# The gate projection's two halves change their place in TensorE's order, in a fused Mamba-2 and product-key expert kernel

## The reference

```python
x = layernorm(x + mamba2(x))       # in-projection, convolution, state-space scan, gate, out-projection
x = layernorm(x + peer(x))         # product-key retrieval of 64 experts per token out of 4096
# mamba2: z, xBC, dt = split(u @ W_in); xBC = silu(conv4(xBC)); y = ssd(x * dt, A * dt, B, C) + D * x
#         y = rmsnorm(y * silu(z)) * norm_scale; out = y @ W_out
# peer:   h = silu(x @ W_up.T + b_up) @ W_down.T + b_down          (width 2048, then 256)
#         q = h @ W_q.T; sim = q . keys; top 8 of 64 per head and half; top 8 of the 8 x 8 sums
#         z = silu((h . down_embed[idx]) * softmax(scores)); out = sum(z * up_embed[idx])
```

## Time and profile before

| | |
|---|---|
| runs | 3216.73, 3226.48, 3239.93 us; median 3226.48 |
| profiled execution | 3229.48 us, its span 3227.5 us |
| busy share | PE 90%, DVE 88%, POOL 70%, ACT 52% |
| mean granted TensorE clock | 0.959 |

### The profile page before, as it was taken

One profiled execution on the slowest core, in us unless ns is written; L12 is line 12 of the kernel. 1 busy time (PEld: TensorE's weight loads), 2 busy tenths in 40 slices (PEclk: granted clock), 3 DMA queues, 4 the chain that ended last, 5 costly groups with the idle time before them and its releaser, 6 DMA issues.

```text
span 3227.5 us, 50404 instructions
## 1 busy us (share of the span) xinstructions
PE 2906.3 (90%) x13856; PEld 1939.0 (60%) x13856; DVE 2840.0 (88%) x10664; ACT 1672.4 (52%) x4833; POOL 2251.4 (70%) x2056
## 2 busy tenths in 40 slices
PE   8899999999998999999998999999999999999864
PEld 8665566665556666556666655666665566665441
DVE  0579999899999999999999999999999999999986
ACT  0546554555555555555555565555555554555521
POOL 0047777777777777777777777777777777777776
PEclk9999999999999999999999999999999999999976
DMA  5258888888888888888888888888888888888887
GB/s 189 111 176 276 272 267 275 283 271 276 273 262 270 287 276 273 275 278 257 284 287 274 269 278 277 266 284 282 274 273 273 274 265 283 281 271 273 270 287 252
DMA packets 189354, 857.11 MB, mean 266 GB/s; under 512 B 36176, under 2 KB 39376, under 8 KB 188048
## 3 DMA queue, kind: packets, MB, share of 16 engines
q0 software_dynamic: 163840, 805.44, 76.2%
q1 hardware_dynamic: 19104, 34.87, 3.2%
q10 hardware_dynamic: 6128, 13.60, 1.1%
HBM read 845.38 MB, written 8.39 MB: 265 GB/s over the span
## 4 chain that ended last, share of the span: by engine, by line
DVE 41%; PE 29%; issue 10%; DMA 10%; ACT 7%; POOL 2%; DVEq 0%; POOLq 0%; ACTq 0%; SPq 0%
DVE acc L1053 11%; DVE ring L1034 10%; DMA ring<-embed,idx 9%; PE bank L457 9%; PE bank L416 7%; PE bank L307 4%; DVE xc L866 3%; PE bank L445 3%; POOL ring L262 2%; DVE i L953 2%; PE bank L290 2%; DVE v L946 1%; ACT L587 1%; ACT L676 1%; DVE zp L1040 1%
## 5 line engine op out<-in xcount | busy, mean ns | idle before, releaser
L262 POOL DMA_INDIRECT ring<-embed,idx x2048 | 2250.1, 1099 | 961.5 <-issue 494.6
L1034 DVE SCALAR_TENSOR_TENSOR ring<-ring,hcur 128x256 f32<-128x256 f32 x2048 | 831.2, 421 | 145.7 <-DMA ring<-embed,idx 141.0
L1053 DVE SCALAR_TENSOR_TENSOR acc<-ring,coef,acc 128x512 f32<-128x512 f32 x1248 | 935.3, 749 | 11.1 <-ACT coef L587 10.9
L457 PE MATMUL bank<-ring,diag_c 128*128 128x512 f32 x1536 | 812.9, 652 | 136.4 <-ACT diag_c L583 136.4
L583 ACT ACTIVATE diag_c<-cst,zp 128x128 f32<-128x128 f32 x768 | 278.6, 399 | 909.4 <-DVE zp L1040 877.7
L457 PEld LDWEIGHTS bank<-ring,diag_c 128*128 128x128 f32 x1536 | 289.8, 205 | 451.1 <-ACT diag_c L583 256.4
L416 PEld LDWEIGHTS bank<-zs,w_up 128*128 128x128 f32 x4096 | 470.8, 192 | 51.3 <-issue 31.2
L416 PE MATMUL bank<-zs,w_up 128*128 128x128 f32 x4096 | 476.4, 276 | 0.8 <-ACT zs L685 0.8
L307 PEld LDWEIGHTS bank<-ut,w_in 128*128 128x128 f32 x2560 | 293.6, 193 | 15.4 <-issue 15.4
L307 PE MATMUL bank<-ut,w_in 128*128 128x128 f32 x2560 | 293.9, 277 | 0.5 <-issue 0.5
L587 ACT ACTIVATE coef<-zp 128x3 f32<-128x3 f32 (+3 forms) x576 | 113.7, 197 | 333.9 <-DVE zp L1040 333.5
(11 more groups left out here) (132 smaller groups left out, 3544.8 us busy)
## 6 DMA issues: line engine op xcount, KB each, us to landing
ring<-embed,idx POOLq DMA_INDIRECT x2048, 4.7
ring<-uT SPq DMA_DIRECT2D x4, 2048.0 KB, 10.1
ut<-uT SPq DMA_DIRECT2D x32, 256.0 KB, 6.6
zs<-u SPq DMA_DIRECT2D x32, 256.0 KB, 5.7
out<-acc SPq DMA_DIRECT2D x32, 256.0 KB, 5.5
w_in<-W_in ACTq DMA_DIRECT2D x1, 4608.0 KB, 21.1
w_up<-W_upT ACTq DMA_DIRECT2D x1, 4096.0 KB, 19.1
w_out<-W_out ACTq DMA_DIRECT2D x1, 2048.0 KB, 9.5
```

The source lines that it names most:

```text
L262: pool.indirect_dma_start(out=ring[:, k % RING, :], out_offset=None, in_=embed, in_offset=bass.IndirectOffsetOnAxis(ap=idx[:, half, k:k + ...
L457: pe.matmul(bank[SUM][:, :], diag_c[:, n % DIAGS, :], ring[:, k % RING, DP:ROW], start=(n == 0), stop=(n == len(PE_ROWS) - 1)).then_inc(ro ...
L1034: dve.scalar_tensor_tensor(out=ring[:, k % RING, 0:DP], in0=ring[:, k % RING, 0:DP], scalar=1.0, in1=hcur[:, :], op0=ALU.mult, op1=ALU.mul ...
L1053: dve.scalar_tensor_tensor(out=total, in0=ring[:, k % RING, DP:ROW], scalar=coef[:, k:k + 1], in1=x1[:, :] if n == 0 else total, op0=ALU.m ...
```

## The change

In PE's program the two halves of the gate projection of tile i+1, which stood together behind the key scores and group 13, stand apart and earlier: the first ahead of the turn of h, the second ahead of the key scores. The other engines' programs are the same.

```diff
@@ PE's tile(i, first, ahead) @@
                 down_proj(i, 3, first, ahead)
                 old(10, 11)
+                if ahead:
+                    z_proj(i + 1, 0)
                 turn_h(i, ahead)
                 old(12)
+                if ahead:
+                    z_proj(i + 1, 1)
                 key_scores(i, 0)
                 key_scores(i, 1)
                 old(13)
                 if ahead:
-                    z_proj(i + 1, 0)
-                    z_proj(i + 1, 1)
                     step_sums(i + 1, 0)
                     step_sums(i + 1, 1)
                     step_sums(i + 1, 2)
```

## The result

The changed kernel takes 3364.32 us (median of 4 runs, 3360.86 to 3365.45) against 3225.06 us: ratio 1.0417, 95% interval 1.0389 to 1.0444. It is 139 us slower, where 94 were forecast. The time lies 4 us above the end of the range that was given.

What follows compares the result with a forecast made beforehand. A loop of waits through PE, DVE, ACT and POOL was taken as the bound. DVE's delay plus a clock halfway between middle (+2.1) and low (+4.1) gave +3.1 us over 30 tiles, 93 us: 3320 us, range 3262 to 3360.

Steps and rivals of the forecast that it cites:

- Which wait ends last: A loop through PE, DVE, ACT and POOL sets the tile, not PE's 90% busy time; 94.90 us a tile.
- Step 1: Ahead of the turn of h: 3.43 us of work fills the 3.28 us gap, turn 0 to 0.5 us late.
- Step 2: Turn of h through key scores: the filled gap keeps the clock full, giving back 1.68 us in such a tile.
- Step 3: Second half ahead of the key scores: DVE's top eights end 1.75 us later, at 10.33 us after the turn of h.
- Step 4: Ahead of the fourth step sum: PE idles 5 us for ACT's gate, works 0.9, idles 2 more before the turn of x.
- The sum by PE's order: Tile time added along PE and DVE work: 96.36 us at full clock, 96.97 middle, 99.03 at low clock.
- POOL's loop: The gathers' path through the turn of x: at full clock +1.75 us a tile, later than PE's +1.5, so it counts.
- Step 5: Turn of x to scan's output, clock lowered by the new gap: halfway between middle and low, tile +3.1 us.
- rival B: Low clock in full through the turn of x and group 16, every tile: +4.1 us a tile, 3350 us; 11%.
- Rivals A: Clock stays full at the new gap, only DVE's delay counts: 53 us, 3279 us; 20%.
- C: DVE's delay absorbed by its waits for gathered rows; some 0.5 us a tile stays, 3242 us; 9%.
- D: PE's own work sets the tile, so the filled gap ahead of h is won: 98 us faster, 3128 us; 5%.

Runs made afterwards that it cites:

- f1: Only the gate projection's first half moved, against the kernel before, on a chip with stalls: 3734.26 us, ratio 1.0045.
- f4: Kernel before, order kept, plus an unused copy of the gate projection's first half ahead of the turn of h, on a chip with stalls: 3712.70 us, ratio 0.9999.
- h3: Changed kernel with its new gap filled by seven repeated step sums per tile: 3272.03 us, ratio 1.0144 to the kernel before.

## Why the prediction was right, and where its size was off

*Which wait ends last.* Right. All but 4.9 of the 105.0 us of PE's gap ahead of h were filled and the kernel got slower, since PE's place behind it waits for ACT's gate, ACT for group 15, and DVE for the key scores.

*Step 1, first half ahead of the turn of h.* Right: nothing waits for it, and the gap is 0.15 us in the mean tile.

*Step 2, the clock's gift.* Right as to the place (5.60 us of work behind the turn of h, with 3.43 more in it, ended at 8.97). What was not seen is that the clock can fall at the turn of x as well with only the first half moved (f1) or a copy added (f4). Both traces are of chips with stalls, so whether it would on the chip of the result is not shown.

*Step 3, DVE's delay.* Right: 1.69 us in the tile shown, 1.75 forecast. Its price alone is 46 us (h3), 53 forecast.

*Step 4, the new gap.* Right in length, place and releaser, POOL's wait included. Behind it the parts were wrong and their sum right: 2.08 us of work and 0.89 us of waiting, where 0.9 and 2 were forecast, because the clock was low already in the fourth step sum. The sum by PE's order was the one that held, as PE's 65% of the chain and the missing gap ahead of h show; POOL's loop no longer closes last.

*Step 5, the clock at the new gap.* This is the term that was mis-sized. I took the point halfway between the tiles at 1585 (17.80 us from the turn of x to the scan's output) and at 537 (19.86): 18.83. The tile shown took 1791.81 - 1771.57 = 20.24, a little over the upper bound, and 20.15 is the mean of 30 tiles. So this term was 1.4 us a tile too small. The others gave 0.3 us back: the turn of x started at 20.68 instead of 20.76 us, and from the scan's output to the next turn of h passed 99.12 - 20.68 - 20.24 = 58.20 us, where 54.98 + 3.43 = 58.41 were forecast. The tile took 99.12 us where the forecast's halfway point gives 98.00. Over the 29 tiles between the first and last turn of h that is 33 us of the miss of 45 (139 - 94). Some 9 us more lie outside them, most of it ahead of the first turn of h (262.29 against 253.22 us); the rest is the distance between single profiled executions and the medians.

The sum with the upper bound had given 99.03 us a tile, and that was rival B, to which I gave 11%. That it comes so close to 99.12 is in part luck, since the bound was 0.4 us too low and the other terms 0.3 us too high. The reason for going to the middle was that one tile in thirty looked like that before. Three tiles of the kernel before had a wait of 1.84 us ahead of the turn of x, and the clock fell there in only one, at 537. These are the other two:

```profile
271.88 1.06 PE L333 MATMUL bank<-cst,xc 128*128 128x128 f32 x8 [1.84 <-ACT seg L633]
...
1129.95 1.06 PE L333 MATMUL bank<-cst,xc 128*128 128x128 f32 x8 [1.84 <-ACT seg L633]
```

So a wait of 1.84 us there did not settle where the clock goes. The rows to go by were those of the gap ahead of h: 2.0 to 5.0 us long, it lowered the clock in 26 of 30 tiles, and the new wait of 5.31 us is longer than all of them. By these the low case was to be expected in nearly every tile. Rivals A, C and D are out: the clock did fall, hardly anything was absorbed (DVE's waits for gathered rows went from 141.0 to 136.8 us), and no PE time was won.

The rule on gaps between bursts of matmuls (the Trainium skill, TensorE: Matmul & The Clock Gate, section Why this matters for your kernels) agrees with the runs in which the gap was filled: with the gap full of repeated work the granted clock of the run rises from 0.911 to 0.980 (h3). It spoke for the change at one gap and against it at the other; the second weighed more. As stated there it is about long gaps; the tile of f4 with waits of 0.69 and 1.84 us shows the low clock behind shorter ones too.

## What to carry to other kernels

Work that is moved into a gap does not remove the gap if what follows waits for another engine; look for where the same idle time comes out again, and what runs at the lower clock behind it. Before work is put ahead of a step, ask who waits for that step (here DVE for the key scores, 75.9 us after the change), and not only whether PE is idle near it. Where an idle stretch of PE can't be avoided and the trace shows the clock low behind it, repeating a harmless matmul in it can be worth more than the order of the work: 92 us here, where the place of the second half was worth 71.

## What the runs showed of the hardware

The length of one wait alone did not tell where the granted clock fell. In the kernel before, waits of 1.84 us ahead of the turn of x were followed by the low clock in one tile of three, and waits for h of 3.17 to 3.33 us left the clock full in three tiles (at 537, 1111 and 1585), while it fell in most others. In f4 it fell behind waits of 0.69 and 1.84 us with 1.12 us of work between.

Three chips of four ran the kernel before 15 to 18% slower, with stretches in which PE starts one instruction per 0.7 us and with long waits of ACT for nothing that the profile shows; the cause is open. The same edits moved the time by other amounts there: the change by +2.4% instead of +4.2%, the first half alone with the gap filled by -1.4% instead of -0.8% (here the two intervals overlap). A ratio from one chip isn't a ratio for the other.
